# State kept by TENSOR_REDUCE, steps moved between slots, and 32 attention heads written out in a four-layer kernel

## The reference

```python
# 1 mamba: 512 inner channels, 16 states
xn = layernorm(x) * ln_g + ln_b
x_br, z = split(xn @ W_in)
xb = silu(causal_conv4(x_br) + conv_b)
Bm, Cm = xb @ W_b, xb @ W_c
delta = softplus(xb @ W_delta + b_delta)
h = exp(delta * A) * h + delta * Bm * xb         # over the tokens
y = sum(h * Cm) + xb * Dp
out = (y * silu(z)) @ W_out + x
# 2 mixture of 4 experts, the best 2 of each token by a router
combine = top2(softmax(gelu(x @ rW1 + rb1) @ rW2 + rb2))
out = sum over e of combine[e] * (gelu(x @ We1[e] + be1[e]) @ We2[e] + be2[e])
# 3 attention: 16 heads of 16 channels in each sequence; q, k and v are projections of x;
#   cross is built from k, v and small weights
attn = softmax((q @ k.T + q_stp @ cross.T) * temp)
out = (attn @ v) @ Wo.T + bo
# 4 feed-forward
out = relu(x @ W1 + b1) @ W2 + b2
```

## Time and profile before

| | us |
|---|---|
| median of 3 runs | 3741.58 |
| the profiled execution | 3739.99 |
| its span, first to last instruction | 3738.2 |
| TensorE busy | 3365.4 (90%) |
| VectorE busy | 2957.0 (79%) |
| ScalarE busy | 2222.1 (59%) |
| GpSimd busy | 1527.4 (41%) |

### The profile page before, as it was taken

How to read it: one execution, slowest core, us unless ns; L and a number is a source line. 1 busy time by engine, 2 the same in 40 slices (tenths; PEclk the granted TensorE clock), 3 DMA queues, 4 the chain that set the end, 5 groups by cost and what they waited for, 6 DMA issues and landing times. The chain is left out here.

```text
span 3738.2 us, 48756 instructions
## 1 busy us (share of the span) xinstructions
PE 3365.4 (90%) x14561; PEld 1574.6 (42%) x14561; DVE 2957.0 (79%) x3571; ACT 2222.1 (59%) x3640; POOL 1527.4 (41%) x1294
## 2 busy tenths in 40 slices
PE   4239999898999899899979999999999999998998
PEld 2015545555555546555623333233233233333666
DVE  5998898989889898975458888888788888887344
ACT  5345666665666665542147777777777777776221
POOL 3998889989889888991010000000000000000110
PEclk8669999999999999999989999999999999999999
DMA  3011213132221213133120000000000000001010
GB/s 107 31 40 48 71 60 105 62 100 70 80 85 64 79 62 100 61 103 108 43 89 19 19 19 18 19 18 18 12 19 19 19 19 19 19 19 35 23 34 28
DMA packets 111205, 183.07 MB, mean 49 GB/s; under 512 B 14623, under 2 KB 84663, under 8 KB 102393
## 3 DMA queue, kind: packets, MB, share of 16 engines
q1 hardware_dynamic: 110969, 180.13, 15.3%
HBM read 153.99 MB, written 26.09 MB: 48 GB/s over the span
## 5 line engine op out<-in xcount | busy, mean ns | idle before, releaser
L1935 DVE TENSOR_REDUCE tile_max<-ps 128x1 f32<-128x1024 f32 x1028 | 1211.2, 1220 | 250.6 <-PE ps L1726 248.1
L1876 ACT ACTIVATE probs<-ps 128x512 f32<-128x512 f32 x2056 | 1116.2, 598 | 372.2 <-PE ps L1740 346.4
L1478 POOL TENSOR_TENSOR vals<-vals,c_sb 128x512 f32<-128x512 f32 x512 | 674.4, 1348 | 154.1 <-DVE state L1279 154.1
L1740 PE MATMUL ps<-stacks 101*128 101x512 bf16 x2056 | 708.8, 383 | 13.6 <-ACTq L1883 12.4
L1273 DVE TENSOR_TENSOR_SCAN vals<-stacks,state,ps 128x512 f32<-128x512 f32 x512 | 655.1, 1279 | 80.6 <-POOL heads_v L1489 23.9
L1489 POOL TENSOR_TENSOR heads_v<-heads_v,vals 128x512 f32<-128x512 f32 x512 | 654.5, 1310 | 8.7 <-issue 0.2
L1726 PE MATMUL ps<-stacks 99*128 99x512 bf16 x2056 | 615.3, 380 | 0.0
L231 POOL COPY heads_v<-vals 128x256 f32 (+1 forms) x32 | 12.6, 400 | 1342.5 <-PE ps L1750 1320.0
L1750 PE MATMUL ps<-probs,heads_v 128*32 128x512 f32 x4096 | 546.4, 605 | 3.3 <-issue 3.3
L734 PE MATMUL ps<-x1T,e_w 128*128 128x512 f32 x1024 | 471.5, 606 | 43.1 <-ACT hid L1046 41.7
L1740 PEld LDWEIGHTS ps<-stacks 101*128 101x128 bf16 x2056 | 198.2, 96 | 650.0 <-ACT probs L1876 431.6
(11 more groups left out here) (200 smaller groups left out, 3115.2 us busy)
## 6 DMA issues: line engine op xcount, KB each, us to landing
e_w<-in_e_w SPq DMA_DIRECT2D x64, 1024.0 KB, 7.1
c_sb<-scratch_c SPq DMA_DIRECT2D x128, 256.0 KB, 3.4
stacks<-scratch_q SPq DMA_DIRECT2D x210, 64.0 KB
stacks<-scratch_k SPq DMA_DIRECT2D x210, 64.0 KB
scratch_q<-parts SPq DMA_DIRECT2D x16, 384.0 KB, 4.4
scratch_k<-parts SPq DMA_DIRECT2D x16, 384.0 KB, 4.4
xr<-scratch_x SPq DMA_DIRECT2D x10, 512.0 KB, 4.2
xn_tok<-in_x SPq DMA_DIRECT2D x8, 512.0 KB, 4.9
```

Of the source, the lines that this page charges most:

```text
L1478: last = nc.gpsimd.tensor_tensor(h[:, n % 2, m, :], h[:, n % 2, m, :], c_sb[:, n % C_RING, :], ALU.mult)
L1740: mm(ps[:, S_BANK[i], :], ks[0:K_ALL, j, step * P:(step + 1) * P], qs[0:K_ALL, j, qc * CH:(qc + 1) * CH], start=True, stop=True).then_inc( ...
L1876: fn(probs[:, step % 2, qc, :], ps[:, S_BANK[i], :], ACT.Exp)\
L1935: v.tensor_reduce(tile_max[:, t, half:half + 1], ps[:, slot(side):slot(side) + PAIR, :].rearrange("p a n -> p (a n)"), AX.X, ALU.max).then ...
```

## The change

It has these parts.

1. `keep_state` is a TENSOR_REDUCE (max) over the last column, read twice by a broadcast, with no factor. It is left out in the last chunk of a sequence, and at the fifth chunk `clear_state` sets the states to zero; the counts in the waits follow.
2. `norm1_stats` goes from the middle of slot 2 to the end of slot 1. ScalarE's `gates` loses a wait on `out_mm`.
3. TensorE's `next_b` goes ahead of the other matmuls of slots 11, 12, 13 and 14.
4. In slots 7 and 9 (`DECAYS_LAST`) ScalarE's `decays(i, n + 1)` come behind the gelus. `logit_exps` goes from slot 6 to slot 7 behind them, `weigh` from the end of slot 6 to the end of slot 7; `down` of expert 0 gets a wait on `router_steps`.
5. `scale("ln0")` goes from slot 11 to 12 on GpSimd, ScalarE's `norm0` from 12 to 13, ahead of `copy_delta(f, 3)`.
6. The 32 heads are written out on every engine, with constants in place of registers. The work for heads 32 and 33 is left out (maxima from step 8 of head 30, scores and exponentials of head 32). The first chunk's output projection, norm and turn are put into head 31. The loads of x2's first two chunks are issued ahead of the heads.

```diff
             def scan(c, n, m):
                 if m == 0:
                     at_least(dve, s["y_added"], c * NS + n - 1)
+                if n == 0 and m == 0 and c > 0 and c % CB == 0:
+                    dve.wait_ge(s["state_cleared"], c // CB)
...
             def keep_state(c, n):
-                keep = cols[:, bass.ds(COL_AT["keep"] + c + 1, 1)]
                 dve.wait_ge(s["h_ready"], (c * NS + n + 1) * DB)
-                v.tensor_scalar(state[:, n, :], h[:, n % 2, :, CH - 1], keep, None, ALU.mult)\
+                v.tensor_reduce(state[:, n, :], h[:, n % 2, :, CH - 1:CH].to_broadcast([P, DB, 2]), AX.X, ALU.max)\
                     .then_inc(s["state_kept"], 1)
+
+            def clear_state(c):
+                dve.wait_ge(s["h_ready"], c * NS * DB)
+                v.memset(state[:], 0.0).then_inc(s["state_cleared"], 1)
...
-                        keep_state(i, n)
-
+                        if (i + 1) % CB:
+                            keep_state(i, n)
+
+                    if n == 1 and inside(m):
+                        norm1_stats(m)
...
-                    if n == 6 and inside(m):
-                        weigh(m)
...
+                    if n == 7 and inside(m):
+                        weigh(m)
```

TensorE, first block:

```diff
                     if n == 11:
+                        next_b(i, n)
                         if inside(m):
                             turn_weights(m)
                             up(m, 2, 1)
-                        next_b(i, n)
...
                     if n in (12, 13):
+                        next_b(i, n)
                         for part in range(2):
                             if inside(f):
                                 project_delta(f, 2 * (n - 12) + part)
                             if inside(m):
                                 down(m, 2, n - 12, (part,))
-                            if part == 0:
-                                next_b(i, n)
                     if n in (14, 15):
+                        if n == 14:
+                            next_b(i, n)
                         if inside(m):
                             up(m, 3, n - 14)
-                        if n == 14:
-                            next_b(i, n)
```

ScalarE and GpSimd, first block:

```diff
-                        if n + 1 < NS and n != 3:
+                        if n + 1 < NS and n not in (3,) + DECAYS_LAST:
                             decays(i, n + 1)
...
-                    if n == 6 and inside(m):
-                        logit_exps(m)
...
+                    if n in DECAYS_LAST and inside(i):
+                        decays(i, n + 1)
+                    if n == 7 and inside(m):
+                        logit_exps(m)
...
-                    if n == 11 and inside(i + 2):
+                    if n == 12 and inside(i + 2):
                         scale("ln0", i + 2)
```

TensorE, attention (VectorE's and ScalarE's follow it):

```diff
+            step_of(0, 0)
+            step_of(0, 1)
+            for u in range(heads):
+                values(u, 0)
+                for step in range(2, KT):
+                    step_of(u, step)
+                    if step == TURN_STEP and u + 1 < heads:
+                        turn_max(u + 1)
+                    values(u, step - 1)
+                    if u == heads - 1 and step == 4:
+                        pe.wait_ge(s["weights"], 96)
+                        turn_o(0)
+                    if u == heads - 1 and step == 8:
+                        project_o(0)
+                    if u == heads - 1 and step == 13:
+                        turn_x3(0)
+                step_of(u + 1, 0)
+                values(u, KT - 1)
+                step_of(u + 1, 1)
+                if u == heads - 1:
+                    pe.wait_ge(s["x3T_ready"], 1)
+                turn_values(u)
+            pe.wait_ge(s["probs_ready"], heads * PER_HEAD)
+            pe.wait_ge(s["max_read"], turn[0])
```

On VectorE `stage_o(0, 0)`, `norm3(0)` and `stage_o(1, 1)` stand ahead of head 31's `normalise`; on ScalarE `copy_o(0)` follows step 5 of head 31 and `copy_x3(0)` step 14. On SP:

```diff
+            load_x2(0, 0)
+            load_x2(1, 1)
+            for u in range(heads):
+                if u + 1 < heads:
+                    load_neg(sp, sh, scr, s["passed_sp"], u + 1, (u + 1) % ROT)
+                if u + 3 < heads:
                     wait_alone(sp, s["passed_sp"], s["scores_mm"], u * PER_HEAD + 1)
-                    load_stack(sp, sh, scr, (u + 3) & (HEADS - 1), (j + 3) % ROT)
+                    load_stack(sp, sh, scr, u + 3, (u + 3) % ROT)
```

More of the change, by code:

```diff
@@ L239 @@
 C_RING = 2
+DECAYS_LAST = (7, 9)
 SIDE = [6, 7, 1]
@@ L1163, in iteration @@
                         soft_log(f, 0)
+                    if n == 13 and inside(i + 2) and not first(f):
+                        norm0(i + 2)
+                    if n == 13 and inside(f):
                         copy_delta(f, 3)
-                    if n == 12 and inside(i + 2) and not first(f):
-                        norm0(i + 2)
                     if n == 1 and first(i):
@@ L1393, in iteration @@
                 for n in range(NS):
+                    if n == 0 and inside(i) and i > 0 and i % CB == 0:
+                        clear_state(i)
                     if inside(i):
@@ L1772, in step_of @@
+            def step_of(u, step):
+                if u >= heads:
+                    return
                 if step == 0:
[L1773 to L1782 removed]
@@ L1802, in _ @@
-            with pe.Fori(0, batches) as b:
-                for quad in range(quads):
-                    four_heads(b * quads + quad)
+                    pe.wait_ge(neg_loaded[u % ROT], 16 * (u // ROT + 1))
+                scores(u, step, 0)
+                next_max(u, step, 0)
+                scores(u, step, 1)
+                scores(u, step, 2)
+                next_max(u, step, 1)
+                scores(u, step, 3)
             def turn_o(c):
@@ L1850, in down @@
                 last.then_inc(s["down_mm"], 1)
-            pe.wait_ge(s["weights"], 96)
-            pe.wait_ge(s["probs_ready"], heads * PER_HEAD + 2 * STEP + CREDIT)
-            pe.wait_ge(s["max_read"], M_BASE + heads * M_PER_HEAD + FOLD_USE + 1)
-            turn_o(0)
-            project_o(0)
-            turn_x3(0)
+            step_of(0, 0)
[22 more added lines that the diff above has]
+            pe.wait_ge(s["max_read"], turn[0])
             with pe.Fori(0, chunks - 1) as c:
@@ L1914, in hidden @@
                         .then_inc(s["hid_ready"], 1)
-            copy_o(0)
-            copy_x3(0)
+            exps(0, 0)
+            exps(0, 1)
+            for u in range(heads):
+                for step in range(2, KT):
+                    exps(u, step)
+                    if u == heads - 1 and step == 5:
+                        act.wait_ge(s["weights"], 96)
+                        copy_o(0)
+                    if u == heads - 1 and step == 14:
+                        copy_x3(0)
+                exps(u + 1, 0)
+                copy_values(u)
+                exps(u + 1, 1)
             with act.Fori(0, chunks - 1) as c:
@@ L2003, in norm4 @@
                            ysum[:], ln_tmp, s["passed_dve"])
-            stage_o(0, 0)
-            norm3(0)
-            stage_o(1, 1)
+            step_of(0, 0)
+            step_of(0, 1)
+            for u in range(heads):
+                for step in range(2, KT):
+                    step_of(u, step)
+                    if u + 1 < heads:
+                        if step == TURN_STEP - 1:
+                            row_maxima(nc, dve, sh, turn[0])
+                        if step == TURN_STEP:
+                            use = turn[0]
+                            negate(nc, dve, sh, ps[0:KT, next_slot(), 0:P], use, u + 1)
+                step_of(u + 1, 0)
+                step_of(u + 1, 1)
+                if u == heads - 1:
+                    stage_o(0, 0)
+                    norm3(0)
+                    stage_o(1, 1)
+                normalise(u)
             with dve.Fori(0, chunks - 1) as c:
```

206 lines of the change are left out of this document (63 added, 143 removed).

## The result

The changed kernel takes 3641.96 us (median of 4 runs, 3641.42 to 3645.86), the kernel before beside it 3739.34 us. The ratio is 0.9737, 95% interval 0.9722 to 0.9753. The forecast was 3646. The profiled execution after took 3645.86 us, with a span of 3644.1 and a mean granted clock of 0.963 (before 0.956).

A forecast was written before the change was run, and what follows sets the result against it. Three nearly full engines bound middle chunks, with TensorE deciding the gain; TensorE alone bounds attention. Chunks' 59.6 us plus heads' 35.6 make 95 us off the profiled 3739.99, so 3646 against the runs; range 3610 to 3688.

The forecast's parts named there:

- The state: Kept state in the chunks: a reduce takes 0.17 us, so VectorE gives back 68 us, 8.6 a chunk.
- rival D: The state's reduce waits for GpSimd as TENSOR_SCALAR did; chunks live on the moved steps alone, 3671 us; chance 0.06.
- the smallest decides: Chunks' sum: of what VectorE, GpSimd and TensorE could give, TensorE's 59.6 us in 7 chunks is the gain.
- B's broadcasts: Slots 11 to 14 of a chunk: earlier issue is worth most of 7.7 us a chunk to VectorE, nothing to TensorE.
- Gelus ahead of decays: Slot 9 of a chunk: TensorE's 1.3 us wait for a gelu's bank goes, 9 us in 7 chunks.
- A: The forecast itself: TensorE sets the chunks' pace, 3646 us; chance 0.48.
- C: Chunks: the three engines loosen one another, GpSimd's waits go and the gate is earlier; chunks give 91 us, 3615; chance 0.25.
- B: Chunks: TensorE doesn't speed up but waits elsewhere instead; chunks give 15 us, 3691 us; chance 0.17.
- E: Slots 7 and 9: decays behind gelus come late for the scans; slower, 3767 us; chance 0.04.
- (a): Attention, where the loop over heads starts again: writing it out saves 5 us, and straight code costs nothing visible.
- (b): Heads 30 and 31: 24 steps without maxima matmuls save 13 us, less 3 exposed by the first chunk's work: 10 net.
- (c): From the last copy of values to up(0): 25.6 us become 5, saving 20.6, if x3's norm ends inside head 31.

The follow-up runs named there:

- Experiment 8: Only B's broadcasts of slots 11 to 14 issued sooner on TensorE, in the kernel before; 3712.93 us, ratio 0.9933.
- the first experiment: The changed kernel with the attention block of before (loops, heads 32 and 33, first chunk's projection behind the heads); 3670.3 us, ratio 0.9815.
- experiment 2: The kernel before with only the attention block of the change; 3711.8 us, ratio 0.9925.

## Why the prediction was right, and where it wasn't

The two profiled executions differ by 94.1 us, where the sum was 95. It came out so near because the chunks gave 6 us more than their term and the heads 11 less, with 4 us from stages that I had at nothing. That these offset one another is luck; what was right is that both halves count, the chunks the more, and most of the waits of TensorE and VectorE that would go.

**The state.** The duration is as taken, 0.161 us for 0.17, and rival D is out. The Trainium skill's page SBUF — State Buffer, section Who interferes with whom, has a tensor_reduce never contending with GpSimd on this chip; the spread of 160 to 163 ns agrees. "VectorE gives back 68 us" holds for these rows alone; VectorE as a whole gave back 48.5 us in the stretch. That the state's saving is worth little by itself held in the kernel before (10 us alone, 3 on top of the broadcasts), but "the smallest decides" gave it nothing at all, and it is 10 to 15 us in the finished kernel.

**x1's statistics.** 39.1 us were expected (26.9 of wait, 12.2 of clock). The wait shrank by 24.7 and the group's busy time by 12.7 (71.4 to 58.7 us), so both rows did what the step said. Yet the part is worth 18 to 25 us: with it undone, TensorE's wait for x1's sum is 24.7 us longer and all its idle time only 9.1 us, since the router's wait for gelus falls from 13.8 to 1.1 us. With the statistics early TensorE comes to the router's banks sooner than the gelus have emptied them. The residual, named as next to be late, was so once: VectorE waited 1.4 us for its DMA, TensorE 2.2 us.

**B's broadcasts.** This is the step that failed: "worth most of the 7.7 us a chunk to VectorE and nothing to TensorE". VectorE's side was right, 53.9 to 3.4 us. But I looked only at what the broadcast itself makes TensorE wait for, not at what a VectorE held up by it makes TensorE wait for afterwards. Experiment 8 shows it in the kernel before: 9.1 us of the wait for an expert's reading, 6.2 us of the gate and 2.9 us of gelus go from TensorE, 22.0 us of idle time in all, and the time falls by 25 us. (The 11.5 us for an expert's reading I had counted under gelus, as going "because VectorE is earlier"; in the changed kernel 6.6 us of it are left.) In the changed kernel the part is worth 22 to 29 us, of which a single profile gives only 7.6 to waits; the rest is in busy time, and how it comes about is open.

**Gelus ahead of decays.** 9 us were taken; the part is worth 13 to 19. TensorE's waits for gelus fell by 15.5 us (41.7 to 26.2), of which 10.5 by this part (36.7 with it undone). But 13.8 us came up at the router's banks, and with the part undone those were 14.5, so they aren't its doing: they are the price of the earlier statistics, as just seen. Table loads fell from 130 to 102 on L948 and L1041, and ScalarE is busy for 820 us in the stretch instead of 857; I had not priced that.

**The clock.** 12.2 us were priced, in the group behind x1's sum, and it gave 12.7. Over the profiles of unchanged chunk code this group takes 69.7 to 76.4 us before, and 57.6 and 58.7 after, so the fall is clear of noise. The experts' group gave 7.4 more that weren't priced; it varies from 471.5 to 481.6 us with the code unchanged, so that this is the change's doing is less sure. The router's group, behind its new wait, took 3.7 us more (58.3 to 62.0).

**The rivals.** A's sum was near (waits 47.4 predicted, 44.9 measured) with the parts wrongly credited. C's argument, that GpSimd's and VectorE's waits free the gate, is right in kind: the gate's wait went from 8.6 to 1.6 us. Its size, 91 us, is out, and so is its premise that GpSimd's waits go: those for VectorE's state and scans are still 90.6 us (70.0 + 20.6), where the state's and the statistics' were 153.7. B is out by the first experiment. E's 12.0 us of waits for decays appeared, and the part still paid.

**The heads.** (a) Restart: 5 expected, 5.9 lost before and 0.27 left (nothing in experiment 2). "Straight code costs nothing visible" was wrong: 0.28 us a head, 7.7 us over the 28 distances that lie neither at the restart nor at the end, more than the 5.4 that the restart's head became shorter. So writing the loop out gains nothing by itself; what it pays for is the special code of the last two heads. (b) The end: 10 us expected, 5.6 measured (from the exponentials of step 8 of head 30 to the last copy, 72.94 before, 67.35 after). ScalarE's timeline after:

```profile
3300.49 2.06 ACT L1866 ACTIVATE probs<-ps 128x512 f32<-128x512 f32 x4 [0.39 <-PE ps L1736]
3302.95 2.06 ACT L1866 ACTIVATE probs<-ps 128x512 f32<-128x512 f32 x4 [0.39 <-PE ps L1736]
...
3329.50 2.06 ACT L1866 ACTIVATE probs<-ps 128x512 f32<-128x512 f32 x4 [1.31 <-PE ps L1736]
...
3343.29 2.06 ACT L1866 ACTIVATE probs<-ps 128x512 f32<-128x512 f32 x4 [3.94 <-PE ps L1736]
...
3356.49 2.06 ACT L1866 ACTIVATE probs<-ps 128x512 f32<-128x512 f32 x4 [1.31 <-PE ps L1736]
...
3362.82 0.60 ACT L1871 ACTIVATE av<-ps 128x512 f32<-128x512 f32 x1 [1.29 <-PE ps L1746]
```

A step takes 2.46 us, 2.06 of work and 0.39 of hand-over, where I took 2.3. The three pieces put into head 31 stand out as 1.31, 3.94 and 1.31 us: above the usual 0.39 that is 5.4 us, and I left 3 exposed. These are the two terms of (b) that were too hopeful. (c) From the last copy (3362.82) to up(0) (3366.43) there are 3.6 us in place of 25.6: 22.0 saved, 20.6 expected. The norm ran from 3343.0 to 3350.2 us, 7.2 us for my 7, well inside head 31:

```profile
3343.01 1.22 DVE L1959 TENSOR_TENSOR x<-ps,x3b 128x1024 f32<-128x1024 f32 x1 [21.86 <-PE ps L1790]
...
3348.84 1.38 DVE L88 TENSOR_SCALAR x<-x,lnf_mv,lnf_r 128x256 f32<-128x256 f32 x4
```

From the first head's RECIPROCAL to the last's the two kernels take 1462.4 and 1457.6 us: 4.8 gained, which is 5.4 at the restart and 7.1 in the last two heads, less the 7.7.

## What to carry to other kernels

Where two engines are both about 90% busy and feed each other, price the removal of a wait by which waits of the other engine stand behind the waiting instruction in its queue, not only by what the moved instruction waits for. The same edit (the state's) measured anywhere from 3 to 15 us, depending on what else was still late, so such parts are judged together. Before a few microseconds of busy time are put down to an edit, compare profiles of unchanged code: here TensorE's busy time in the chunks moved by 14 us between them and its idle time by 6. Moving work behind other work paid in two slots and lost 28 us in four, so such a list is to be tried slot by slot, by the waits on both sides of it.

## What the runs showed of the hardware

- A four-column TENSOR_SCALAR from strided columns takes 229 to 2212 ns (median 545) where GpSimd is busy beside it. With the other parts of the change in place the same form had a median of 231 ns, a mean of 529 (662 before) and a maximum of 1807, though GpSimd was as busy (1251.5 us of the stretch, 1253.3 before). That it depends on where GpSimd stands just then is a reading of this, not shown by itself. The TENSOR_REDUCE in its place took 160 to 163 ns throughout.
- Straight code with constants made each head 0.28 us longer than the loop with registers, 0.15 for TensorE and 0.13 for ScalarE with VectorE. Plain steps are the same, 2.84 us. The difference sits at the two turns of a head: at that of the maxima ScalarE's next step begins 3.50 us after the last in place of 3.34, and behind that of the values ScalarE waits 1.58 us in place of 1.46 for the next scores. Why, no view shows.
- A wait of TensorE can cost more than its length. The 16 matmuls behind the wait for x1's sum took 715 ns each on average with it, 613 without it and 733 with the wait put back. Over the whole stretch 20.4 us of busy time went with 44.9 us of waits, and the granted clock rose from 0.97 to 0.98 of full speed.
- The clock moves TensorE's busy time by 14 us, over one and the same chunk code in four profiles (1295.0 to 1309.3 us at 0.97 to 0.96).
